# Moving the second key transposes of an attention stage behind the projection or the mixing product

## What is computed

```
x = x + (einsum('bsi,bio->bso', x, W0[id]) + b0[id])          # an expert per batch
x = x + (x W1^T + lora(x, adapter[b]))                         # dense layer with low-rank adapters
q, k, v = x Wq^T, x Wk^T, x Wv^T                               # 8 query heads, 4 key heads, width 64
q, k = rope(rms(q)), rope(rms(k))
k_blocks, v_blocks = old caches with the new k, v written into them (block table, 16 tokens a block)
scores = q . k_all * SCALE, only the last 256 positions up to each token's own
p = softmax(scores);  o = p . v_all
x = x + o Wo^T
x = x + (w3[subject] mixes the 64 tokens of a batch, + b3[subject])
```

## Time and profile before

| what | value |
|---|---|
| median of three runs | 966.55 us (964.24 to 967.04) |
| the profiled execution, its time | 962.48 us |
| its span | 960.7 us |
| granted TensorE clock, mean | 0.996 |
| busy: TensorE products, its weight loads | 931.3 us, 687.7 us |
| busy: VectorE, ScalarE, GpSimd | 604.0 us, 383.8 us, 512.8 us |
| phase two, first instruction to the end of the span | 520.8 to 960.7 us |

### The profile page before, as it was taken

One profiled execution on the slowest core, in us unless ns is written; L12 is line 12 of the kernel. 1 busy time (PEld: TensorE's weight loads), 2 busy tenths in 40 slices (PEclk: granted clock), 3 DMA queues, 4 the chain that ended last, 5 costly groups with the idle time before them and its releaser, 6 DMA issues.

```text
span 960.7 us, 22134 instructions
## 1 busy us (share of the span) xinstructions
PE 931.3 (97%) x6253; PEld 687.7 (72%) x6253; DVE 604.0 (63%) x1788; ACT 383.8 (40%) x1061; POOL 512.8 (53%) x469
## 2 busy tenths in 40 slices
PE   6899999999999999999997899999999999999997
PEld 4566767667676666767666678877878788878785
DVE  5434344666565644346554777778777787777874
ACT  2121212212122121221223656666666666666662
POOL 1245454544536467664566666555666556565530
PEclk9999999999999999999999999999999999999999
DMA  9888887786776868777734666666666666666741
GB/s 300 272 279 289 292 299 233 262 279 229 257 244 235 279 215 272 233 240 277 265 131 140 192 197 179 192 211 179 201 193 184 211 215 191 197 191 204 220 124 46
DMA packets 105162, 212.48 MB, mean 221 GB/s; under 512 B 29563, under 2 KB 52056, under 8 KB 96930
## 3 DMA queue, kind: packets, MB, share of 16 engines
q1 hardware_dynamic: 71042, 145.54, 45.1%
q0 software_dynamic: 25088, 57.74, 20.5%
q10 hardware_dynamic: 8992, 8.73, 2.8%
HBM read 204.39 MB, written 33.86 MB: 248 GB/s over the span
## 4 chain that ended last, share of the span: by engine, by line
PE 91%; SPq 3%; DMA 2%; issue 1%; DVE 1%; ACT 1%; POOL 0%; DVEq 0%; POOLq 0%; ACTq 0%
PE banks L587 11%; PE banks L802 9%; PE banks L705 9%; PE banks L753 8%; PE banks L790 7%; PE banks L626 6%; PE banks L634 6%; PE banks L636 6%; PE banks L776 6%; PE banks L795 4%; PE banks L730 4%; PE banks L838 3%; PE banks L695 3%; PE banks L710 3%; PE banks L597 2%; PE banks L770 1%
## 5 line engine op out<-in xcount | busy, mean ns | idle before, releaser
L546 POOL DMA_INDIRECT ring<-new_rows,idx x128 | 129.4, 1011 | 82.2 <-DVE big L1278 55.5
L458 POOL TENSOR_TENSOR rms<-ss,neg_half 128x12 f32<-128x12 f32 x31 | 70.8, 2284 | 165.3 <-DVE ss L1184 165.3
L930 ACT ACTIVATE big<-big,neg_max 128x320 f32<-128x320 f32 x256 | 141.3, 555 | 4.2 <-DVE neg_max L1242 4.0
L1242 DVE CUSTOM_DVE_ANT_0 big<-banks,mask 128x320 f32<-128x320 f32 x256 | 114.6, 485 | 32.8 <-PE banks L753 30.7
L587 PE MATMUL banks<-ring 128*64 128x512 f32 x512 | 118.8, 607 | 2.0 <-DMA ring<-in_w 2.0
L871 ACT ACTIVATE x2t_hi<-banks 128x512 fp32r<-128x512 f32 x32 | 19.1, 598 | 235.5 <-PE banks L597 235.5
L920 ACT ACTIVATE kt<-banks 128x384 f32<-128x384 f32 x128 | 62.0, 485 | 95.6 <-PE banks L731 95.5
L587 PEld LDWEIGHTS banks<-ring 128*64 128x64 f32 x512 | 34.6, 138 | 81.6 <-issue 80.4
L535 POOL DMA_INDIRECT ring<-new_rows,idx x64 | 61.5, 961 | 53.2 <-PE banks L776 48.7
L753 PE MATMUL banks<-kt,q_in 64*128 64x128 f32 (+2 forms) x768 | 86.8, 358 | 1.3 <-ACT kt L920 1.3
L1278 DVE TENSOR_SCALAR big<-big,recip 128x320 f32<-128x320 f32 x256 | 86.0, 398 | 2.3
(11 more groups left out here) (169 smaller groups left out, 1980.8 us busy)
## 6 DMA issues: line engine op xcount, KB each, us to landing
ring<-in_w SPq DMA_DIRECT2D x62, 1024.0 KB, 6.0
ring<-in_xt SPq DMA_DIRECT2D x32, 256.0 KB, 2.7
x_in<-in_x SPq DMA_DIRECT2D x32, 256.0 KB, 5.4
bias_in<-in_b SPq DMA_DIRECT2D x64, 128.0 KB, 5.4
x_dram<-x SPq DMA_DIRECT2D x32, 256.0 KB, 5.0
q_dram<-q_t ACTq DMA_DIRECT2D x32, 256.0 KB, 2.3
new_rows<-kv_out SPq DMA_DIRECT2D x32, 256.0 KB, 4.8
q_in<-q_dram SPq DMA_DIRECT2D x64, 128.0 KB
```

The source lines that it names most:

```text
L546: pool.indirect_dma_start(out=kv[:, s, c, :], out_offset=None, in_=new_rows, in_offset=bass.IndirectOffsetOnAxis(ap=idx[:, b, 1 + c:2 + c] ...
L930: nc.scalar.activation(prob[:, s % 2, g * NK:(g + 1) * NK], sm[:, s % 2, g, :], ACT.Exp, bias=neg_max[:, s % 2, g:g + 1], scale=-1.0, accu ...
L1242: V.tensor_tensor_reduce(sm[:, s % 2, g, :], ps_s[g], mask[:, s % 2, k0:k0 + NK], 1.0, 3.0e38, ALU.add, ALU.min, accum_out=neg_max[:, s % ...
```

## The change

In a step of phase two the call that transposes the second key half of batch b + 1 moves from place 5 to a place between 6 and 7. Its three transposes, their wait on `kt_ready` and their signal `kt_done` go with it. Nothing else is edited.

```diff
@@ phase_two of the tensor program
                     transpose_probs()
                 if second_half and behind_probs:
                     project(range(DC // 2, DC), ps_x).then_inc(wo_done, 1)
-                if on(b, -1, NB):
-                    transpose_keys(b + 1, j + (s == KV_SLOTS - 1), (s + 1) % KV_SLOTS, 1)
                 if first_half:
 
                     pe.wait_ge(ot_ready, 2 * pair + 2)
@@
                         pe.wait_ge(x3_ready, pair + 1 + i)
                         nc.tensor.matmul((ps_mix[i] if is_last(pair) else ps_x)[:, n0:n1], bd[:, pair_s, :], x3[:, pair_s, n0:n1],
                                          start=True, stop=True).then_inc(l3_done, 1)
+                if on(b, -1, NB):
+                    transpose_keys(b + 1, j + (s == KV_SLOTS - 1), (s + 1) % KV_SLOTS, 1)
                 if on(b, 1, NB) and not behind_probs:
                     values()
```

## The result

The changed kernel takes 975.23 us (973.12 to 979.76, 4 runs); the kernel before takes 966.04 (964.24 to 967.04, 4 runs, one more than in the 966.55 of the prediction). The ratio is estimated from all runs, and is 1.0102 with a 95% interval of 1.0058 to 1.0146: slower by 1.0%. The two medians differ by 9.2 us. The profiled execution took 973.32 us, with a span of 971.5 against 960.7.

A forecast was written before the change was run, and what follows sets the result against it. TensorE was taken to bound the kernel, with a product always running in settled phase two. Odd steps 7.4, even steps 0.3 and step 3 1.3 make 9.0 us on the 966.55 median: 975.5, range 970.5 to 979.5.

The forecast's parts named there:

- Odd steps, the wait for `x4_ready`: Projection's first load waits for VectorE's final addition: 0.27 us in 26 odd steps, 0.12 in 3; 7.4 us.
- Even steps: Mixing product's load 0.02 to 0.06 late for `x3_ready`, values about 0.01 late in 28 steps; 0.3 us in all.
- Who waits for the keys: Later `kt_done` of the second key half delays neither ScalarE's copy, the scores nor GpSimd's gathers that matter; no cost.
- Neighbours on the array: A transpose now directly precedes the values; the 0.09 us gap at the tile change stays, term zero, bounds 2.7 either way.
- Step 3: Once: ScalarE's key copy, ahead of three exponentials, comes later and delays step 4's values; +1.3 us, between 0.5 and 1.5.
- absorbed: Rival: VectorE and ScalarE set the pace, so the step pair stays at 13.27 us; about 968 us, chance 0.06.
- Faster: Rival: the 0.09 us gap at the tile change goes in 60 steps, -5.4 us; 962.5 us, chance 0.03.
- More than the hole: Rival: GpSimd's gather over VectorE's scaling in odd steps delays the next mask, 0.3 us a pair; about 984 us, chance 0.07.

The follow-up runs named there:

- step3_old: The changed kernel, but in step 3 alone the second key half's transposes stay ahead of the projection; 975.6 us, ratio 1.0111 (1.0072 to 1.0149) to the kernel before.

## Why the prediction was right, point by point

**Odd steps, the wait for `x4_ready`**: right, by mechanism, count and place. The rows of step 27 show the load behind the addition, and the traces show the same in the loop's 26 steps by more and in steps 5, 7 and 61 by less. The size was 0.27 and is 0.29 (6.197 to 6.489); 0.12 became 0.14. The difference is mostly the latency from the addition's end to the load, put at 0.09 between 0.07 and 0.11: it is 0.115 in all of them, the upper of the two rows, which was the one with VectorE as producer and a separate wait ahead of the load. Term: 7.4, measured 8.0.

**Even steps**: 0.3 forecast, 0.8 measured, inside the bounds. (The forecast counted 28 even steps; there are 30, from 4 to 62, which changes 0.02 us.) Most cost nothing or 0.01 (7.07 to 7.09), but seven of the loop's steps, 10, 18 and so on to 58, are 7.15, step 56 is 7.12, and the unrolled ones 6, 60 and 62 are 7.14. In those the wait for `x3_ready` stands as an instruction of its own and the load starts 0.115 behind the addition's end; in the others it sits on the weight load, 0.053 behind. These are two latencies, where I had taken one.

**Who waits for the keys**: ScalarE and the scores, right: the copy starts at 711.23, as soon as its exponentials allow, and ends 0.6 ahead of the scores. GpSimd's first gather started later than I said, at 711.63 and not at 710.9: between the transposes' end (710.77) and the gather lie 0.86 us, which I had taken as 0.14. It cost nothing, since the gather behind it waits for VectorE's probabilities anyway.

**Neighbours on the array**: right. From the start of the last transpose's product to that of the values' first load and product it is 0.20 (710.50 to 710.70), 0.11 for the transpose and 0.09 of gap, the same gap as behind a projection. The Trainium skill, page TensorEngine Tiling (Array Packing), section Key Properties, says that changing the tiling mode drains TensorE. The trace agrees, in that the gap at the change is 0.09 in both orders.

**Step 3**: the mechanism is right, as `step3_old` shows. Term 1.3, measured 1.05: the first exponential of step 4 starts 2.34 us behind the scores before and 3.31 after, so 1.0 later and not 1.3: the first mask comes 1.2 later behind the scores, and the exponential behind it had 0.2 of slack that I took for none.

**Sum**: 9.0 forecast; the terms measure 9.9 in the profiled executions, and the medians differ by 9.2. That 975.5 was forecast and 975.23 measured is partly luck: terms mis-sized by +0.6, +0.5 and -0.25 partly cancel, and the interval of the ratio allows anything from 5.6 to 14 us. I had put the profiled execution's 4.1 us below the median down to phase one and its loads; no run shows that. What the traces do show is that the start of step 3 alone moves by almost 5 us between them. Of the rivals, *absorbed* needed odd steps of 6.20 or shorter even steps: neither is there. *Faster* needed the gap to go: it stayed. *More than the hole*, GpSimd's gather over VectorE's scaling, was half right: with the gather from 711.63 over it the scaling of step 27 takes 1.49 us in place of 1.27, and over the whole kernel the mean of L1278 goes from 398 to 417 ns. But the first mask of step 28 still waits 0.25 us for the scores, so nothing reached TensorE: even steps grew by 0.03 and not by 0.3.

## What to carry to other kernels

A step that moves within a saturated engine's program costs nothing as work, but ask what it was covering where it stood: here 0.33 us of transposes hid a wait for a bank that VectorE was still reading. Compare the end of every producer with the slot of the load that waits for it, in the timeline, before and after the move; the sum of count times lateness gave the traced loss to within a microsecond. The lateness belongs to the chip as well: on the slower one the same comparison failed, since VectorE's additions came 0.7 us later. When such a wait is uncovered, the cheaper repair may be on the producer's side: the addition fitted into time in which VectorE was idle. No run here is faster than the kernel before beyond its interval, and none of the terms promised it, since in the kernel before TensorE has a product running in all of the 338 us of the earlier trace rows.

## What was unexpected

The price of TensorE's wait for VectorE depends on its form: 0.053 us from the addition's end to the weight load when the wait sits on the load, 0.115 when it is an instruction of its own, in every step with such a wait, to within 0.01 us, on both kinds of chips. For ScalarE as the producer gave a third value, 0.07. The same line of the program had one form or the other by its place in the unrolled loop body.

The two kinds of chips differed by 4 to 5% for the same kernel (964.5 against 1006.9 and 1010.1 us). The kernel before wasn't traced on the slower one. In the traces that there are, the first keys of phase two are transposed at 520.3 to 522.6 us on the faster chips and at 519.3 to 525.9 on the slower one, so the difference arises in phase two. And on the slower one two changes that the other traces price at 0.7 and 1.7 us cost 6 to 12.
